# Gated delta rule on one core: places of six small steps and of a recurrence's factors

## The chip, the core and the metric

One NeuronCore of a Trainium2 chip runs the whole program, all in fp32. The metric is the time of one execution on the device in microseconds; three executions of the kernel before were timed. TensorE (PE), VectorE (DVE), ScalarE (ACT), GpSimd (POOL) and SyncE each have a queue of their own and meet only through semaphores.

## What is computed

The reference is a chain of four residual blocks: a gated delta-rule attention, a mixture of experts, a banded attention, and a two-layer local attention. Only the first is touched. Its core, for 4 sequences of 1024 tokens, 16 heads, and 64 keys by 64 values:

```
def step(S, inp):
    qt, kt, vt, at, bt = inp
    err = jnp.einsum('bhij,bhj->bhi', S, kt) - vt
    S = at[..., None] * S - bt[..., None, None] * (err[..., None] * kt[:, :, None, :])
    o = jnp.einsum('bhij,bhj->bhi', S, qt)
    return (S, o)
...
mu = o.mean(-1, keepdims=True)
var = ((o - mu) ** 2).mean(-1, keepdims=True)
o = (o - mu) / jnp.sqrt(var + EPS) * ln_w + ln_b
g = jax.nn.sigmoid(x @ Wg.T).reshape(Bb, Tt, H, DV)
o = (o * g).reshape(Bb, Tt, H * DV)
return o @ Wo.T
```

## The kernel before

`DeltaRule` cuts the 1024 tokens into 32 segments (`SEG` = 32), each into two chunks (`CK` = 16 steps), each chunk into halves (`HC` = 8). A chunk g = 2s + ch of segment s goes like this:

- TensorE projects, makes the products of keys and queries among themselves (Gram), and what the past gives: `pe_past_state` (from the state) and `pe_past_chunk` (L691, from the chunk before). VectorE turns the result into `P2` (L1292), multiplies its first four columns (`HAND` = 4) by the heads' factors `dk` (L1297, L1363 for the second half) and takes them from the values (L1302; the second half adds, L1366).
- VectorE then does the steps t = 1 to 15: a product of the history `H` with a Gram row in PSUM (L1327), a decay (L1331, with the gates' copy `abank` in PSUM) and a sum (L1333). For t from 4 to 7 the decay is GpSimd's (`pool_history`).
- Between the halves stands `dve_cross`: VectorE turns the history (L1348), TensorE multiplies it (`pe_cross`, L709), and VectorE turns the product (L1361). While TensorE works, VectorE does other things: the mean or the deviation of the segment before (L1271), the gates' turn `dve_gates` (L1247, first chunk) or the Gram's turn (L1263, second chunk), and the output's turn (L1281).
- `dve_state` ends the chunk: it turns the history (L1389), which releases L691 for the next chunk, and makes the last output (L1391 to L1398).
- The state sum `dve_add` (L1375, two instructions) stands in the first chunk at step t = 4, the reciprocal (L1276) in the second chunk at t = 11.

Each engine's queue is an order written out by hand (`tensor`, `scalar`, `gpsimd`, `vector`). TensorE's projections share two PSUM banks as a ring: `take` waits until what is two places ahead in the ring has been evacuated. The mean and the deviation use bank 4. The time rows (`pe_time_rows`, L604, two halves) stand at the head of a segment, ahead of the gate's projections; ScalarE evacuates them at L871. GpSimd makes `dk` in `pool_prepare` (L1063, L1065), behind four state decays (L1012) and much else; ScalarE copies Gram rows (`act_gram_bank`, L891, L892) and gates (`act_gate_rows`, L880) to PSUM banks 2 and 3 when the last product of a chunk (L1391) has been made.

## Time and profile before

| | |
|---|---|
| median of three timed executions | 3798.79 us (3794.1 to 3808.33) |
| the profiled execution | 3802.33 us, of which 3800.5 us from its first to its last instruction |
| mean granted TensorE clock | 0.926 |
| PE busy | 3221.9 us (85%) |
| DVE busy | 2951.2 us (78%) |
| ACT busy | 1981.8 us (52%) |
| POOL busy | 2230.6 us (59%) |

The delta rule's recurrence fills the first 2260 us; the other blocks follow. Busy time counts instructions on an engine, not its waits. In a row of the trace, the number in square brackets is the idle time of the engine just before the instruction, and what ended it. A clock of 1.00 is 2.4 GHz and 0.50 is 1.2 GHz; a value between is a mean over a stretch.

### The profile page before, as it was taken

How to read it: one execution, taken by the hardware profiler on the slowest of the kernel's cores; microseconds unless marked ns; L12 is line 12 of the kernel's file. 1: busy time of each engine (PE TensorE's matmuls, PEld its weight loads, DVE VectorE, ACT ScalarE, POOL GpSimd, SP SyncE). 2: the span in 40 equal slices, each digit the busy share in tenths (PEclk: the TensorE clock that was granted, in tenths of full speed). 3: DMA queues.
4: the chain of work that ended last, by engine and by line, in shares of the span. 5: the costliest groups of instructions: out<-in, count | busy, mean ns of one | idle time of the engine just before them, and what ended most of it. 6: DMA issues, size and time to landing. Idle time of an engine off the chain costs nothing. (4 is left out here: it accounts for less than half of the span.)

```text
span 3800.5 us, 141833 instructions
## 1 busy us (share of the span) xinstructions
PE 3221.9 (85%) x61117; PEld 2418.8 (64%) x61117; DVE 2951.2 (78%) x6533; ACT 1981.8 (52%) x4486; POOL 2230.6 (59%) x2825
## 2 busy tenths in 40 slices
PE   3688898888888888889888845689999799889989
PEld 2567676767767676767677644556666477656765
DVE  4488888888888888889888942178888688738884
ACT  2434444444444444444444323258887699629972
POOL 1377778787877777787877744320101388418860
PEclk7889999999999998999999966899999899999999
DMA  2111111111111111111111115100000012101111
GB/s 76 34 43 41 35 52 30 52 34 45 42 45 42 45 41 37 50 30 49 31 40 40 40 31 149 40 1 2 2 2 2 23 35 44 29 20 29 43 32 28
DMA packets 156019, 141.03 MB, mean 37 GB/s; under 512 B 64976, under 2 KB 108236, under 8 KB 155138
## 3 DMA queue, kind: packets, MB, share of 16 engines
q1 hardware_dynamic: 153090, 129.25, 12.5%
q8 instruction: 482, 7.90, 0.9%
...
q14 instruction: 143, 1.17, 0.1%
...
## 5 line engine op out<-in xcount | busy, mean ns | idle before, releaser
L1327 DVE TENSOR_TENSOR a_tmp<-a_h,banks 128x128 f32<-128x128 f32 (+6 forms) x896 | 435.7, 486 | 28.7
L1333 DVE TENSOR_REDUCE a_h<-a_tmp 128x64 f32<-128x128 f32 (+6 forms) x896 | 432.1, 482 | 8.8
L1012 POOL TENSOR_TENSOR a_st<-a_st,a_ab 128x512 f32<-128x512 f32 x252 | 313.6, 1277 | 0.0
L820 ACT ACTIVATE a_kq<-banks 128x512 f32<-128x512 f32 (+2 forms) x160 | 88.3, 552 | 426.6 <-PE banks L556 426.6
L2207 ACT ACTIVATE c_s<-c_s,c_low 128x384 f32<-128x384 f32 (+1 forms) x512 | 266.3, 579 | 19.1 <-DVE c_low L2151 13.6
L1027 POOL TENSOR_TENSOR a_h<-a_h,a_a 128x128 f32<-128x128 f32 (+3 forms) x256 | 141.3, 552 | 228.4 <-DVE a_h L1333 225.6
L2252 POOL TENSOR_TENSOR c_qm<-c_qT,c_heads 128x512 f32<-128x512 f32 x32 | 33.3, 1040 | 396.2 <-PE banks L2076 395.9
L2151 DVE CUSTOM_DVE_ANT_0 c_s<-banks,c_band 128x384 f32<-128x384 f32 (+1 forms) x512 | 245.4, 517 | 23.5 <-PE banks L2076 23.5
L556 PE MATMUL banks<-a_xseg,a_w_q 128*128 128x128 f32 x2048 | 253.4, 278 | 9.0 <-ACT a_kq L820 8.5
L556 PE MATMUL banks<-a_xseg,a_w_k 128*128 128x128 f32 x2048 | 243.0, 276 | 17.1 <-DMA a_xseg<-xn 17.1
L556 PEld LDWEIGHTS banks<-a_xseg,a_w_q 128*128 128x128 f32 x2048 | 235.8, 190 | 21.6 <-ACT a_kq L820 15.4
L556 PEld LDWEIGHTS banks<-a_xseg,a_w_k 128*128 128x128 f32 x2048 | 237.1, 193 | 17.9 <-issue 17.6
L829 ACT ACTIVATE a_va<-banks 128x512 f32<-128x512 f32 x128 | 136.8, 1095 | 208.5 <-PE banks L569 208.0
L569 PE MATMUL banks<-a_w_v,a_xseg 128*32 128x512 f32 x2048 | 242.1, 610 | 0.5 <-issue 0.3
L2090 PE MATMUL banks<-k_ident,c_s 128*128 128x128 f32 x1408 | 216.6, 283 | 28.7 <-ACT c_pt L2214 15.8
L691 PE MATMUL banks<-a_wt,a_gn 32*32 32x64 f32 x8064 | 152.1, 237 | 102.1 <-DVE a_wt L1389 98.9
L709 PE MATMUL banks<-a_wt,a_gx 32*32 32x64 f32 x8192 | 164.3, 244 | 84.9 <-DVE a_wt L1348 72.3
L2090 PEld LDWEIGHTS banks<-k_ident,c_s 128*128 128x128 f32 x1408 | 154.3, 142 | 119.8 <-ACT c_s L2207 113.6
L691 PEld LDWEIGHTS banks<-a_wt,a_gn 32*32 32x32 f32 x8064 | 139.1, 120 | 134.5 <-DVE a_wt L1389 129.7
L709 PEld LDWEIGHTS banks<-a_wt,a_gx 32*32 32x32 f32 x8192 | 151.3, 125 | 93.1 <-issue 89.1
L2588 ACT ACTIVATE d_S<-d_S,d_low 128x128 f32<-128x128 f32 x512 | 199.2, 399 | 19.0 <-DVE d_low L2653 18.7
L2437 PE MATMUL banks<-d_wqkv,d_hT 128*128 128x512 f32 x384 | 199.0, 633 | 11.2 <-DVE d_rot L2635 6.7
...
## 6 DMA issues: line engine op xcount, KB each, us to landing
a_ab<-decays SPq DMA_DIRECT2D x512, 128.0 KB, 3.1
d_Vs<-d_V SPq DMA_DIRECT2D x128, 128.0 KB, 2.4
...
a_xrow<-in_L_attn_x SPq DMA_DIRECT2D x128, 16.0 KB, 1.8
x<-a_xrow SPq DMA_DIRECT2D x128, 16.0 KB, 1.8
...
```

What stands on the lines that cost most here:

```text
L556: t = e.matmul(b[:, m * SW:(m + 1) * SW].rearrange("p (b t) -> p b t", b=NB), self.wT[n][:, j, ct * P:(ct + 1) * P], xs[:, :, off:off + SE ...
L569: t = e.matmul(b[bi * SEG:(bi + 1) * SEG, :], xs[:, bi, off:off + SEG], self.wT[n][:, j, part], start=(j == 0), stop=(j == taps - 1))
L691: t = e.matmul(pb[rows, at:at + DK], self.Gn[1 - ch][rows, 8 * par + ct, :], self.Wt[rows, x:x + 2, :].rearrange("p h i -> p (h i)"), star ...
L709: t = e.matmul(xb[rows, at:at + DK], self.Gx[rows, 8 * par + ct].rearrange("p t z -> p (t z)"), self.Wt[rows, x:x + 2, :].rearrange("p h i ...
L1012: e.tensor_tensor(sv, sv, self.ab[:, 8 * n:8 * n + 8, :], ALU.mult).then_inc(*self.s_decay.at((g, n)))
L1327: e.tensor_tensor(prod, both, gram, ALU.mult).then_inc(*step.at((g, t, "product")))
L1333: e.tensor_reduce(self.results(ch, t), prod, AX.X, ALU.add).then_inc(*step.at((g, t, "w")))
L2090: t = e.transpose(b[:, j * P:(j + 1) * P], self.S[u % self.NS][:, j * P:(j + 1) * P], self.c.ident[:])
L2151: e.tensor_tensor_reduce(out=self.S[u % self.NS][:, 0:w], in0=self.c.bank(r)[:, 0:w], in1=self.W.band[:, m0:m0 + w], scale=-HD ** -0.5, sc ...
L2207: e.activation(s[:, 0:w], s[:, 0:w], ACT.Exp, scale=-1.0, bias=self.low[u % self.NS][:, 0:1]).then_inc(*self.s_exp.at(u))
L2437: e.matmul(b, self.hT[:, g * P:(g + 1) * P], self.W.wqkv[:, z * INNER:(z + 1) * INNER], start=True, stop=True).then_inc(*self.s_proj.at((g ...
L2588: t = e.activation(s, s, ACT.Exp, scale=-1.0, bias=self.low[g % 2][:, par, r:r + 1], accum_out=self.rows[g % 2][:, par, r:r + 1])
```

## The change

What it does, in the order of the diff:

- `H` has its parts in another order, and the results of a step are written output first. Gram rows lie in bank 2 in the order that goes with it, and only the half of each row that is read is copied.
- The factors for the first four columns of each half go to PSUM: ScalarE copies them from `dk` to the free halves of bank 2 (`act_factors`, two instructions for each chunk, ahead of the Gram rows). VectorE's four small instructions each take one operand from PSUM, and the two multiplications also write to PSUM (`scaled`, a free part of bank 3), so that VectorE waits for the gates' copy already there. GpSimd's `pool_prepare` waits for the factors' copy in place of VectorE's multiplications.
- The time rows stand in two places of the second chunk: half 0 behind the next segment's Gram product and ahead of `pe_cross`, half 1 between the past state and the second half of the value projection; the last segment has none.
- The mean's product takes a place in the bank ring and no longer waits for the state sum.
- On VectorE, the state sum stands behind the first chunk's L1348, the gates' turn at the end of the first chunk's `dve_state`, and the reciprocal behind the Gram's turn in the second chunk's `dve_cross`.

```
@@ -474,8 +474,8 @@
...
             self.H = sb("h", [P, 32, 2 * SEG + 2 * CK])
-            self.W = [self.H[:, :, ch * SEG:(ch + 1) * SEG] for ch in range(NCK)]
-            self.Wx, self.O = self.H[:, :, 2 * SEG:2 * SEG + CK], self.H[:, :, 2 * SEG + CK:]
+            self.O, self.Wx = self.H[:, :, 0:CK], self.H[:, :, CK + 2 * SEG:]
+            self.W = [self.H[:, :, CK + ch * SEG:CK + (ch + 1) * SEG] for ch in range(NCK)]
             self.ab = sb("ab", [P, R, DK])
@@ -501,6 +501,7 @@
...
+        self.s_factor = sig("factor")
         self.s_p2, self.s_prep, self.s_step, self.s_wt, self.s_st, self.s_o = (
@@ -511,12 +512,17 @@
...
-        self.gbank = c.bank(2).rearrange("p (t z j) -> p t z j", z=2, j=CK)
+        self.gbank = c.bank(2).rearrange("p (r j) -> p r j", j=CK)
+        self.factor = [self.gbank[:, 2 * HC * h:2 * HC * (h + 1), HC - HC * h:CK - HC * h].rearrange("p r (i t) -> p r i t", t=HAND)
+                       for h in range(2)]
+        self.scaled = c.bank(3)[:, HAND * 32:2 * HAND * 32].rearrange("p (r i t) -> p r i t", i=2, t=HAND)
         self.abank = c.bank(3).rearrange("p (t i) -> p t i", i=32)
...
-        return ch * (SEG + CK) if t <= HAND or t >= HC or (t - HAND) % 2 == 0 else 2 * SEG
+        return CK + (ch * (SEG + CK) if t <= HAND or t >= HC or (t - HAND) % 2 == 0 else 2 * SEG)
@@ -525,8 +531,8 @@
...
-        w, o = self.first_column(ch, t + 1) + t, 2 * SEG + CK + t - 1
-        return self.H[:, :, w:o + 1:o - w].rearrange("p i z -> p z i")
+        w, o = self.first_column(ch, t + 1) + t, t - 1
+        return self.H[:, :, o:w + 1:w - o].rearrange("p i y -> p y i")
@@ -538,7 +544,7 @@
...
         if n >= 2:
-            q.wait_ge(self.s_evac, self.ring[n - 2])
+            q.wait_ge(self.s_moment if self.ring[n - 2][0] == "mean" else self.s_evac, self.ring[n - 2])
         return self.c.bank(n % 2)
@@ -616,16 +622,13 @@
...
-        b = self.c.bank(4)
-        if s + 1 < self.nseg:
-            if which == "mean":
-                q.wait_ge(self.s_st, (s, 3))
-            else:
-                q.wait_ge(self.s_p2, 2 * s + 3)
         if which == "mean":
+            b = self.take(q, ("mean", s))
             q.wait_ge(self.s_o, 2 * s + 1)
         else:
-            q.wait_ge(self.s_moment, ("mean", s))
+            b = self.c.bank(4)
+            if s + 1 < self.nseg:
+                q.wait_ge(self.s_p2, 2 * s + 3)
             q.wait_ge(self.s_squared, s)
@@ -656,7 +659,6 @@
...
             q.wait_ge(self.s_st, (s - 1, 3))
-            q.wait_ge(self.s_moment, ("mean", s - 1))
         if ch == 0 and s >= 2:
@@ -758,8 +760,6 @@
...
                 self.pe_project_rows(e, q, "a", nxt, 1)
-            for n in range(2):
-                self.pe_time_rows(e, q, s, n)
             if older >= 0:
@@ -792,10 +792,12 @@
...
                     self.pe_next_gram(e, q, s, n)
+                self.pe_time_rows(e, q, s, 0)
             self.pe_cross(e, q, s, 1)
...
                 self.pe_past_state(e, q, g + 2)
+                self.pe_time_rows(e, q, s, 1)
                 self.pe_project_rows(e, q, "v", nxt, 1)
@@ -884,12 +886,24 @@
...
         s, ch = divmod(g, 2)
-        js = slice(ch * CK, (ch + 1) * CK)
+        c0, rows = ch * CK, self.g2[:].rearrange("p t z j -> p (t z) j")
         q.wait_ge(self.s_bg, (s, ch))
...
             q.wait_ge(self.s_step, (g - 1, "last", "q"))
-        e.activation(self.gbank[:, 0:CK - 1, 0, :], self.g2[:, 1:CK, 0, js], ACT.Copy)
-        e.activation(self.gbank[:, :, 1, :], self.g2[:, :, 1, js], ACT.Copy).then_inc(*self.s_gbank.at(g))
+        e.activation(self.gbank[:, 0:2 * HC - 2, 0:HC], rows[:, 1:2 * HC - 1, c0:c0 + HC], ACT.Copy)
+        e.activation(self.gbank[:, 2 * HC:2 * CK - 1, HC:], rows[:, 2 * HC + 1:, c0 + HC:c0 + CK], ACT.Copy).then_inc(*self.s_gbank.at(g))
+    def by_pairs(self, x):
+        return x.rearrange("p (r i) t -> p r i t", i=2)
+    def act_factors(self, e, q, g):
+        q.wait_ge(self.s_dk, (g, 1))
+        if g:
+            q.wait_ge(self.s_step, (g - 1, "last", "q"))
+        for h in range(2):
+            t = e.activation(self.factor[h], self.by_pairs(self.dk[:, :, h * HC:h * HC + HAND]), ACT.Copy)
+        t.then_inc(*self.s_factor.at(g))
@@ -944,6 +958,7 @@
...
         self.act_cross_gram(e, q, 0)
+        self.act_factors(e, q, 0)
         self.act_gram_bank(e, q, 0)
@@ -954,8 +969,6 @@
...
                     self.act_project_rows(e, q, "a", nxt, half)
-            for n in range(2):
-                self.act_time_rows(e, q, s, n)
             if older >= 0:
@@ -967,6 +980,7 @@
...
                     self.act_project(e, q, "q", nxt, part)
+            self.act_factors(e, q, g + 1)
             self.act_gram_bank(e, q, g + 1)
@@ -981,13 +995,15 @@
...
                     self.act_next_gram(e, q, s, n)
+                self.act_time_rows(e, q, s, 0)
             if old >= 0:
...
                 self.act_cross_gram(e, q, nxt)
-                for half in range(2):
-                    self.act_project_rows(e, q, "v", nxt, half)
-            if more:
+                self.act_project_rows(e, q, "v", nxt, 0)
+                self.act_time_rows(e, q, s, 1)
+                self.act_project_rows(e, q, "v", nxt, 1)
+                self.act_factors(e, q, g + 2)
                 self.act_gram_bank(e, q, g + 2)
@@ -1035,7 +1051,7 @@
...
     def past_part(self):
-        return self.H[:, :, SEG:SEG + CK]
+        return self.H[:, :, CK + SEG:CK + SEG + CK]
@@ -1044,7 +1060,7 @@
...
         q.wait_ge(self.s_wm, 2 * s + 1)
-        e.tensor_tensor(self.past_part(), self.H[:, :, 0:CK], by, ALU.mult).then_inc(*self.s_past.at(s))
+        e.tensor_tensor(self.past_part(), self.W[0][:, :, 0:CK], by, ALU.mult).then_inc(*self.s_past.at(s))
@@ -1057,9 +1073,8 @@
...
         if g:
-            q.wait_ge(self.s_prep, (g - 1, "mul"))
+            q.wait_ge(self.s_factor, g - 1)
             q.wait_ge(self.s_rest, (g - 1, "late"))
-            q.wait_ge(self.s_mid, (g - 1, "mul"))
         e.tensor_tensor(halves(self.dk[:])[:, :, :, 1:], halves(self.dc[s % 2][:, :, ch * CK:(ch + 1) * CK])[:, :, :, 0:HC - 1],
@@ -1268,7 +1283,8 @@
...
             q.wait_ge(self.s_root, s - 1)
-        e.tensor_reduce((self.mom if which == "mean" else self.var)[:], self.c.bank(4)[:, 0:P].rearrange("p (i t) -> p t i", t=SEG),
+        b = self.held(("mean", s)) if which == "mean" else self.c.bank(4)
+        e.tensor_reduce((self.mom if which == "mean" else self.var)[:], b[:, 0:P].rearrange("p (i t) -> p t i", t=SEG),
                         AX.X, ALU.add).then_inc(*self.s_moment.at((which, s)))
@@ -1292,18 +1308,18 @@
...
         q.wait_ge(self.s_p2, g)
-        q.wait_ge(self.s_dk, (g, 1))
-        first = P2[:, :, 0:HAND, 0]
-        e.tensor_tensor(first, first, self.dk[:, :, 0:HAND], ALU.mult).then_inc(*self.s_prep.at((g, "mul")))
+        q.wait_ge(self.s_factor, g)
+        q.wait_ge(self.s_abank, g)
+        pairs = self.by_pairs
+        e.tensor_tensor(self.scaled, pairs(P2[:, :, 0:HAND, 0]), self.factor[0], ALU.mult).then_inc(*self.s_prep.at((g, "mul")))
         q.wait_ge(self.s_prep, (g, "mul"))
...
             q.wait_ge(step, (g - 2, "last", "o"))
-        e.tensor_tensor(Wc[:, :, c0:c0 + HAND], self.bv[:, :, c0:c0 + HAND], first,
+        e.tensor_tensor(pairs(Wc[:, :, c0:c0 + HAND]), pairs(self.bv[:, :, c0:c0 + HAND]), self.scaled,
                         ALU.subtract).then_inc(*self.s_prep.at((g, "sub")))
...
         q.wait_ge(self.s_gbank, g)
-        q.wait_ge(self.s_abank, g)
         for t in range(1, CK):
@@ -1311,14 +1327,12 @@
...
             both = hist[:, :, lo:t + 1].rearrange("p (o i) j -> p o i j", o=1).broadcast_to([P, 2, 32, t + 1 - lo])
-            gram = self.gbank[:, t - 1, :, lo:t + 1].rearrange("p z (o j) -> p z o j", o=1).broadcast_to([P, 2, 32, t + 1 - lo])
+            gram = self.gbank[:, 2 * t - 2:2 * t, lo:t + 1].rearrange("p y (o j) -> p y o j", o=1).broadcast_to([P, 2, 32, t + 1 - lo])
             if t == lo + 1 and lo:
...
             if t == HAND:
-                if ch == 0 and s:
-                    self.dve_add(e, q, s - 1)
                 q.wait_ge(self.s_rest, (g, "sub", 1))
@@ -1331,13 +1345,11 @@
...
             e.tensor_reduce(self.results(ch, t), prod, AX.X, ALU.add).then_inc(*step.at((g, t, "w")))
-            if ch == 1 and t == 11 and s:
-                self.dve_reciprocal(e, q, s - 1)
...
-        g, x = 2 * s + ch, self.X[:, :, HC:HC + HAND, 0]
+        g, pairs = 2 * s + ch, self.by_pairs
         q.wait_ge(self.s_step, (g, HC - 1, "w"))
@@ -1346,13 +1358,14 @@
...
         e.transpose(self.Wt[:].rearrange("p x i -> p i x"), self.W[ch]).then_inc(*self.s_wm.at(g))
+        if ch == 0 and s:
+            self.dve_add(e, q, s - 1)
         if s:
             self.dve_moment(e, q, s - 1, "dev" if ch else "mean")
-        if s + 1 < self.nseg:
-            if ch:
-                self.dve_gram_rows(e, q, s + 1)
-            else:
-                self.dve_gates(e, q, s + 1)
+        if ch and s + 1 < self.nseg:
+            self.dve_gram_rows(e, q, s + 1)
+        if ch and s:
+            self.dve_reciprocal(e, q, s - 1)
         if ch == 0 and s >= 2:
@@ -1360,10 +1373,10 @@
...
         q.wait_ge(self.s_xt, g)
-        e.tensor_tensor(x, x, self.dk[:, :, HC:HC + HAND], ALU.mult).then_inc(*self.s_mid.at((g, "mul")))
+        e.tensor_tensor(self.scaled, pairs(self.X[:, :, HC:HC + HAND, 0]), self.factor[1], ALU.mult).then_inc(*self.s_mid.at((g, "mul")))
         q.wait_ge(self.s_mid, (g, "mul"))
         q.wait_ge(self.s_rest, (g, "less"))
-        e.tensor_tensor(self.history(ch, HC)[:, :, HC:HC + HAND], self.P2[:, :, HC:HC + HAND, 0], x, ALU.add).then_inc(
+        e.tensor_tensor(pairs(self.history(ch, HC)[:, :, HC:HC + HAND]), pairs(self.P2[:, :, HC:HC + HAND, 0]), self.scaled, ALU.add).then_inc(
             *self.s_mid.at((g, "add")))
@@ -1387,7 +1400,7 @@
...
             e.transpose(self.Wt[:].rearrange("p x i -> p i x"), Wc).then_inc(*self.s_wt.at(g))
-        gq = self.gbank[:, CK - 1, 1, HC:].rearrange("p (o j) -> p o j", o=1).broadcast_to([P, 32, HC])
+        gq = self.gbank[:, 2 * CK - 2, HC:].rearrange("p (o j) -> p o j", o=1).broadcast_to([P, 32, HC])
         e.tensor_tensor(self.tmp[:, 1, :, 0:HC], Wc[:, :, c0 + HC:row], gq, ALU.mult).then_inc(*self.s_step.at((g, "last", "q")))
@@ -1396,8 +1409,8 @@
...
         e.tensor_tensor(o2[:, :, c0:row], self.P2[:, :, :, 1], self.O, ALU.subtract).then_inc(*self.s_o.at(g))
-        if ch and more:
-            self.dve_values(e, q, s + 1)
+        if more:
+            (self.dve_values if ch else self.dve_gates)(e, q, s + 1)
```

## Rows read from the trace of the kernel before

**Rows 1.** Recurrence: length, busy PE, PEld, DVE, ACT, POOL, clock, DMA share, GB/s.
```profile
138.70:2260.00 2121.30, 1821.12 (x47378) 1460.49 (x47367) 1835.58 (x3421) 908.01 (x1673) 1614.13 (x2199) 0.93 0.14 41
```

**Rows 2.** VectorE by line, recurrence: busy us, mean ns | idle before us.
```profile
L1361 DVE STREAM_TRANSPOSE a_cross<-banks 128x1024 f32<-128x1024 f32 x64 | 79.9, 1249 | 127.7 <-PE banks L709 127.7
L1292 DVE STREAM_TRANSPOSE a_p<-banks 128x1024 f32<-128x1024 f32 x64 | 79.3, 1240 | 43.1 <-PE banks L691 43.1
L1302 DVE TENSOR_TENSOR a_h<-a_bv,a_p 128x128 f32<-128x128 f32 x64 | 58.0, 907 | 2.2
...
L1297 DVE TENSOR_TENSOR a_p<-a_p,a_dk 128x128 f32<-128x128 f32 x64 | 39.4, 616 | 2.2
...
L1366 DVE TENSOR_TENSOR a_h<-a_p,a_cross 128x128 f32<-128x128 f32 x64 | 30.9, 483 | 2.2
L1363 DVE TENSOR_TENSOR a_cross<-a_cross,a_dk 128x128 f32<-128x128 f32 x64 | 27.2, 426 | 2.2
...
L1276 DVE RECIPROCAL a_mom<-a_mom 128x32 f32<-128x32 f32 x32 | 11.0, 343 | 0.4 <-ACT a_mom L904 0.4
```

**Rows 3.** VectorE in order of time, one segment: start us, us, [idle before].
```profile
1005.91 1.24 DVE L1247 STREAM_TRANSPOSE a_a<-a_va 128x1024 f32<-128x1024 f32 x1
...
1008.79 1.25 DVE L1361 STREAM_TRANSPOSE a_cross<-banks 128x1024 f32<-128x1024 f32 x1 [0.52 <-PE banks L709]
...
1014.14 0.29 DVE L1331 TENSOR_TENSOR a_h<-a_h,banks 128x128 f32<-128x128 f32 x1
...
1024.38 1.25 DVE L1292 STREAM_TRANSPOSE a_p<-banks 128x1024 f32<-128x1024 f32 x1 [1.39 <-PE banks L691]
...
1032.92 0.62 DVE L1333 TENSOR_REDUCE a_h<-a_tmp 128x64 f32<-128x448 f32 x1
...
1035.02 1.94 DVE L1348 STREAM_TRANSPOSE a_wt<-a_h 128x1024 f32<-128x1024 f32 x1
...
1040.43 1.25 DVE L1361 STREAM_TRANSPOSE a_cross<-banks 128x1024 f32<-128x1024 f32 x1 [2.24 <-PE banks L709]
1041.72 0.90 DVE L1363 TENSOR_TENSOR a_cross<-a_cross,a_dk 128x128 f32<-128x128 f32 x1
...
1056.99 1.25 DVE L1292 STREAM_TRANSPOSE a_p<-banks 128x1024 f32<-128x1024 f32 x1 [0.54 <-PE banks L691]
1058.27 0.91 DVE L1297 TENSOR_TENSOR a_p<-a_p,a_dk 128x128 f32<-128x128 f32 x1
...
1062.42 1.29 DVE L1375 TENSOR_TENSOR a_st<-a_st,banks 128x512 f32<-128x512 f32 x2
```

**Rows 4.** TensorE in order of time, the same segment.
```profile
1006.74 1.99 PE L709 MATMUL banks<-a_wt,a_gx 32*32 32x64 f32 x128
...
1037.11 3.28 PE L709 MATMUL banks<-a_wt,a_gx 32*32 32x64 f32 x128 [2.30 <-DVE a_wt L1348]
...
1053.90 3.04 PE L691 MATMUL banks<-a_wt,a_gn 32*32 32x64 f32 x128 [2.34 <-DVE a_wt L1389]
...
1062.12 2.02 PE L604 MATMUL banks<-k_ident,a_kq 128*32 128x128 f32 x64 [0.50 <-ACT a_va L829]
```

**Rows 5.** Window sums of the two L709 stretches; the clock stands third from the end.
```profile
1006.70:1008.80 2.10, 2.10 (x130) 1.97 (x130) 1.58 (x3) 0.65 (x1) 1.83 (x3) 1.00 0.04 8
1037.10:1040.40 3.30, 3.29 (x132) 3.13 (x136) 1.09 (x1) 0.30 (x1) 3.30 (x4) 0.57 0.02 5
```

**Rows 6.** GpSimd in order of time, second half of the same segment.
```profile
1037.51 4.96 POOL L1012 TENSOR_TENSOR a_st<-a_st,a_ab 128x512 f32<-128x512 f32 x4
...
1054.23 0.31 POOL L1065 COPY a_dk<-a_beta 128x64 f32<-128x64 f32 x1
1056.52 2.51 POOL L1166 TENSOR_TENSOR a_bv<-a_bv,a_beta 128x512 f32<-128x512 f32 x2 [1.99 <-DVE a_bv L1255]
```

**Rows 7.** ScalarE in order of time, the same segment.
```profile
1033.60 0.28 ACT L899 ACTIVATE a_orow<-banks 128x128 f32<-128x128 f32 x1
...
1054.81 0.79 ACT L880 ACTIVATE banks<-a_a 128x96 f32<-128x96 f32 x2
```

More of the change, by code:

```diff
@@ L540, in take @@
         if n >= 2:
-            q.wait_ge(self.s_evac, self.ring[n - 2])
+            q.wait_ge(self.s_moment if self.ring[n - 2][0] == "mean" else self.s_evac, self.ring[n - 2])
         return self.c.bank(n % 2)
@@ L760, in tensor @@
                 self.pe_project_rows(e, q, "a", nxt, 1)
-            for n in range(2):
-                self.pe_time_rows(e, q, s, n)
             if older >= 0:
@@ L886, in act_gram_bank @@
         s, ch = divmod(g, 2)
-        js = slice(ch * CK, (ch + 1) * CK)
+        c0, rows = ch * CK, self.g2[:].rearrange("p t z j -> p (t z) j")
         q.wait_ge(self.s_bg, (s, ch))
@@ L956, in scalar @@
                     self.act_project_rows(e, q, "a", nxt, half)
-            for n in range(2):
-                self.act_time_rows(e, q, s, n)
             if older >= 0:
@@ L987, in scalar @@
                 self.act_cross_gram(e, q, nxt)
-                for half in range(2):
-                    self.act_project_rows(e, q, "v", nxt, half)
-            if more:
+                self.act_project_rows(e, q, "v", nxt, 0)
+                self.act_time_rows(e, q, s, 1)
+                self.act_project_rows(e, q, "v", nxt, 1)
+                self.act_factors(e, q, g + 2)
                 self.act_gram_bank(e, q, g + 2)
@@ L1270, in dve_moment @@
             q.wait_ge(self.s_root, s - 1)
-        e.tensor_reduce((self.mom if which == "mean" else self.var)[:], self.c.bank(4)[:, 0:P].rearrange("p (i t) -> p t i", t=SEG),
+        b = self.held(("mean", s)) if which == "mean" else self.c.bank(4)
+        e.tensor_reduce((self.mom if which == "mean" else self.var)[:], b[:, 0:P].rearrange("p (i t) -> p t i", t=SEG),
                         AX.X, ALU.add).then_inc(*self.s_moment.at((which, s)))
```

92 lines of the change are left out of this document (51 added, 41 removed).

## The prediction

> **What bounds the kernel now.** I read the page's busy shares first, then the recurrence alone. It runs from 138.7 to 2260 us, 2121 us for 32 segments, 66.3 us each, and VectorE is busy 1835.6 us of it, TensorE 1821.1 us and GpSimd 1614.1 us [rows 1]. Next I read VectorE's groups by line, for the idle time ahead of them and for the mean of each. Nearly all of the idle time stands at two lines: 127.7 us ahead of L1361 (turn of the cross product, called X here) and 43.1 us ahead of L1292 (turn of the past product, called P), both released by TensorE. Beside that, four small instructions have means that don't fit their size: L1297, L1302, L1363 and L1366 all handle 128x128, and take 616, 907, 426 and 483 ns [rows 2].
>
> Then one segment in VectorE's order of time, from some 1004 to 1068 us. It has four waits: X in the first chunk 0.52 us, P in the second 1.39, X in the second 2.24, P of the next first chunk 0.54 [rows 3]. TensorE's part of the same stretch shows why the two late ones last: it waits 2.30 us for the turned history and then needs 3.28 us for the 128 small matmuls of L709, which took 1.99 us where no wait stood before them; L691 takes 3.04 us behind a wait of 2.34 [rows 4]. The granted clock was 0.57 in the slow stretch and 1.00 in the quick one, that is, mostly the 1.2 GHz level against the 2.4 GHz level [rows 5]. And the four odd instructions follow GpSimd: L1297 ends at 1059.18, 0.15 us after GpSimd's L1166 pair (1056.52 + 2.51); L1363 ends at 1042.62, 0.15 us after GpSimd's four decays (1037.51 + 4.96) [rows 3, 6]. L1331 on the same 128x128, with one operand in PSUM, took 0.29 us at 1014.14, an ordinary time for it [rows 3]. So the bound is VectorE's own chain, lengthened by TensorE's answers and by GpSimd's hold on it.
>
> **The four small instructions.** All become: one operand in SBUF, one in PSUM (two of them write PSUM too). Nearest row: L1331 at 0.29. The four groups sum to 39.4 + 58.0 + 27.2 + 30.9 = 155.5 us [rows 2]; 256 x 0.29 = 74.2; to gain at most 81.3 us. No arithmetic of the trace writes PSUM from VectorE. Bounds: 0.29 each, or 0.43 each (the next step that these lines show, as in L1366's 483 mean), which would cost 36 us more; I take 0.29, since L1331 has the same size and a PSUM operand.
>
> The Trainium skill speaks against this: "VectorE: DVE Perf Modes", section on the TRN2 errata, gives a PSUM source 120 fixed cycles against 58 for SBUF, an estimate of 0.065 us more for each, 17 us in all. The trace doesn't agree: 0.29 for L1331.
>
> **The waits.** In the first chunk, behind L1348, the state sum (L1375, a pair in 1.29 us) takes the place of the gates' turn (L1247, 1.24 us) [rows 3]. VectorE's cover ahead of X stays 2.75 us; the wait goes because L709 starts on time. Before, the projections ahead of it ran past L1348; the two L604 groups now taken out of this stretch were 2.02 us and 0.50 of waiting for ScalarE [rows 4]. With 0.15 + 1.99 us the product is there before the cover ends. Mean in the bank ring only takes the wait for the state sum off TensorE, which would otherwise stand in front of the mean; its price is that the turn two slots later waits for VectorE's L1271, about 1.5 us behind L1348, while TensorE is still at L709: nothing. Turn 0 does wait about 0.6 us for L1281, which stands behind the state sum; TensorE has about that much to spare before L691.
>
> The gates' turn goes to the end of the first chunk's state step, in the wait of 1.39 us before P: 0.15 left [rows 3]. L691's product is usually there in 2.1 us, in this segment in 2.8, and the cover is now 2.8. Who is behind it: GpSimd's cumulation (first used 7 us later) and the "v" projections' evacuation.
>
> In the second chunk, the reciprocal (L1276, 0.34 us [rows 2]) moves ahead of X, and L604's first half (1.0 us) fills TensorE's wait of 2.30 before L709, the second half part of the 2.34 before L691 [rows 4]. What is left of each is about what TensorE had at other places without the clock falling, so I take 1.99 us for both products. X then comes 2.1 us behind L1348 instead of 3.4. A new wait appears: the evacuation of the time rows now stands on ScalarE ahead of the table load and the square root, so the reciprocal waits about 0.5 us; X starts 1.17 us earlier instead of 1.6.
>
> **What is late next.** From the end of step 6 of the second chunk (1032.92 + 0.62 = 1033.54) to L1297 of the next chunk (1058.27) VectorE now takes 24.73 us [rows 3]. Without 1.17 at X, 0.54 at P and 0.75 at L1363 and L1366 it would take 22.3. But GpSimd runs without a break from the same point to the end of L1065 (1054.54), 21.0 us [rows 6]. In the change ScalarE starts its factor copies only then, two at 0.28 (L899, 128x128), the two halved Gram copies at 0.28, and the gate rows at 0.79 [rows 7]: 1.9 us. VectorE waits for all of them ahead of its first multiplication, since `scaled` lies in the gate rows' bank. 21.0 + 1.9 = 22.9. L1398 still has two operands in SBUF and now falls among GpSimd's instructions; bounds 0 and 0.69, I add 0.4: 23.3. So this stretch goes from 24.73 to 23.3 and not to 21.2, the sum of all its idle and held time: 2.1 us for each segment aren't given back.
>
> On L1398 the Trainium skill, "SBUF — State Buffer", section on the two separate sides, says that whichever of the two engines comes first holds the shared port for its whole instruction. By that rule the 0.4 would be 0.69, 9 us more in all. No row shows L1398 beside GpSimd.
>
> In the first chunk's stretch L1065 is 2 us earlier than needed and ScalarE's chain fits.
>
> **The sum.** Idle 127.7 + 43.1 and held 81.3 make 252 us. Off: 31 x 2.1 = 65 for GpSimd's chain; 9 for the first and last segment, whose waits have no neighbour's work to fill them (an estimate, two segments of 4.7); 4 for what passes the gates' cover; 7 for a lower clock at the first chunk's L709 in a third of the segments (0.15 + 3.28 - 2.75 = 0.7 each, and TensorE now waits ahead of it). 252 - 65 - 9 - 4 - 7 = 167. The profiled execution took 3802.3 us (span 3800.5), 3.5 above the median of 3798.8, so 3802.3 - 167 = **3635 us**. Nothing behind 2260 us is touched.
>
> **Rivals.**
> A. An instruction with one SBUF operand still waits for GpSimd, so the factors in PSUM do nothing. For: GpSimd's decays ran through every chunk and VectorE's transposes of SBUF can't be told from free ones. Against: L1331 at 0.29 amid the decays. The 81 us stay, of which 0.75 a segment (23) lay under GpSimd's chain anyway: 109 us of gain, 3693.
> B. The low clock stays or moves to the first chunk's products. For: TensorE still waits a microsecond at each place. Then the second chunk's stretch takes 24.73 - 0.34 - 0.75 = 23.6 against 23.3, and X and P of the two other places cost 0.7 + 0.35: 1.35 x 31 less the 7 counted, 35 us less: 3670.
> C. GpSimd's chain isn't the limit, because it too is freed of the held instructions and ScalarE needs less: the stretch takes 22.3, 31 us more gain: 3604.
> D. **Slower**: ScalarE's chain behind L1065. Every microsecond that the factor copies take above 0.56 counts in the second chunk's stretch, and in the first chunk's behind a slack of 1.8. With c us more it costs c + c - 1.8, and eats the 5.4 us of gain per segment from c = 3.6, that is, 2.1 us a copy. At c = 4.0 it is 6.2 against 5.4: 25 us slower, 3827. Against: no ScalarE copy of this size takes over 0.28 [rows 7].
>
> **Chances.** Forecast 0.56, A 0.14, B 0.13, C 0.12, D 0.05. The range takes in A, B and C with the ends of the unknown costs: 3598 to 3698. A measurement here can tell about 0.5% (19 us) from no change; faster by more 0.94, within 0.02, slower by more 0.04.
>
> **What would show it.** Right: the means of the four small groups at 290 ns; idle ahead of P near nothing in the second chunk; idle ahead of X under 40 us in all; L709 and L691 at 2 us with clock 1.00; VectorE waiting about 1 us, for ScalarE's gate rows (L880's successor), ahead of the first multiplication of each first chunk. Wrong: means of 400 to 900 (A), X of the second chunk still 2 us late (B), no wait at the first multiplication (C), factor copies over 1 us (D).

## The result

The changed kernel takes 3685.96 us (3683.97 to 3692.4) against 3798.9 us (3794.1 to 3808.33) for the kernel before, a ratio of 0.9699 with a 95% interval of 0.9679 to 0.972: 113 us faster. Its profiled execution spans 3682.8 us, at a mean granted clock of 0.946 where it was 0.926. The forecast was 3635 us, a gain of 164 us against the median, in a range of 3598 to 3698. So the direction and the range held, and 51 us of the gain didn't come.

The recurrence shrank from 2121.3 to 2003.3 us. Window sums of the kernel after over that stretch (length; busy PE, PEld, DVE, ACT, POOL with instruction counts; clock; DMA share; GB/s), which answer [rows 1]:

```profile
138.70:2142.00 2003.30, 1769.59 (x47296) 1411.82 (x47288) 1767.87 (x3421) 919.45 (x1798) 1611.52 (x2199) 0.97 0.15 43
```

VectorE's groups by line in the kernel after, recurrence (busy us, mean ns | idle us before them and what ended it), which answer [rows 2]. L1374 is X, L1308 is P; L1314, L1319, L1376 and L1379 are the four small instructions (L1297, L1302, L1363, L1366 before); L1292 is the reciprocal:

```profile
L1374 DVE STREAM_TRANSPOSE a_cross<-banks 128x1024 f32<-128x1024 f32 x64 | 79.9, 1248 | 62.7 <-PE banks L711 62.3
L1308 DVE STREAM_TRANSPOSE a_p<-banks 128x1024 f32<-128x1024 f32 x64 | 77.6, 1213 | 3.6 <-PE banks L693 3.4
L1411 DVE TENSOR_TENSOR a_o<-a_p,a_h 128x512 f32<-128x512 f32 x64 | 51.5, 804 | 2.2
...
L1314 DVE TENSOR_TENSOR banks<-a_p,banks 128x128 f32<-128x128 f32 x64 | 18.9, 296 | 4.0 <-ACT banks L882 1.9
L1376 DVE TENSOR_TENSOR banks<-a_cross,banks 128x128 f32<-128x128 f32 x64 | 18.9, 296 | 2.2
L1379 DVE TENSOR_TENSOR a_h<-a_p,banks 128x128 f32<-128x128 f32 x64 | 18.4, 287 | 2.2
L1319 DVE TENSOR_TENSOR a_h<-a_bv,banks 128x128 f32<-128x128 f32 x64 | 18.3, 287 | 2.2
L1292 DVE RECIPROCAL a_mom<-a_mom 128x32 f32<-128x32 f32 x32 | 11.3, 353 | 57.1 <-ACT a_mom L918 57.1
```

The four small groups fell from 155.5 to 74.5 us (-81.0), the idle time ahead of P from 43.1 to 3.6 (-39.5), that ahead of X from 127.7 to 62.7 (-65.0). Against them stands a new wait: 57.1 us ahead of the reciprocal, for ScalarE's square root, where it was 0.4. L1411, with both operands in SBUF still, grew by 7.2 us from this row of the kernel before:

```profile
L1398 DVE TENSOR_TENSOR a_o<-a_p,a_h 128x512 f32<-128x512 f32 x64 | 44.3, 692 | 2.2
```

-81.0 - 39.5 - 65.0 + 56.7 + 7.2 = -121.6; the recurrence is 118.0 us shorter. In this sum 56.7 is the rise of the reciprocal's wait (57.1 less 0.4).

One segment of the kernel after in VectorE's order of time (start us, us, [idle before and what ended it]), which answers [rows 3]:

```profile
985.51 2.00 DVE L1360 STREAM_TRANSPOSE a_wt<-a_h 128x1024 f32<-128x1024 f32 x1
...
990.22 0.35 DVE L1292 RECIPROCAL a_mom<-a_mom 128x32 f32<-128x32 f32 x1 [1.49 <-ACT a_mom L918]
...
991.28 1.25 DVE L1374 STREAM_TRANSPOSE a_cross<-banks 128x1024 f32<-128x1024 f32 x1 [0.72 <-PE banks L711]
...
1007.71 0.30 DVE L1314 TENSOR_TENSOR banks<-a_p,banks 128x128 f32<-128x128 f32 x1
...
1021.26 1.25 DVE L1374 STREAM_TRANSPOSE a_cross<-banks 128x1024 f32<-128x1024 f32 x1 [0.71 <-PE banks L711]
...
1036.41 1.21 DVE L1308 STREAM_TRANSPOSE a_p<-banks 128x1024 f32<-128x1024 f32 x1
```

Both P come without a wait. But X of the second chunk starts 3.77 us behind the end of L1360 (987.51 to 991.28), where it was 3.47 (1036.96 to 1040.43 [rows 3]) and should have become 2.3, that is 3.47 less the 1.17 of the prediction. TensorE in the same segment shows why:

```profile
986.80 1.08 PE L610 MATMUL banks<-k_ident,a_kq 128*32 128x128 f32 x32
987.82 1.42 PE L711 MATMUL banks<-a_wt,a_gx 32*32 32x64 f32 x87
990.45 0.77 PE L711 MATMUL banks<-a_wt,a_gx 32*32 32x64 f32 x41 [1.21 <-issue]
...
1003.94 1.99 PE L693 MATMUL banks<-a_wt,a_gn 32*32 32x64 f32 x128 [0.92 <-DVE a_wt L1402]
...
1010.00 0.57 PE L737 MATMUL banks<-a_wt,a_kt 32*64 32x64 f32 x22 [1.14 <-issue]
...
1019.20 1.99 PE L711 MATMUL banks<-a_wt,a_gx 32*32 32x64 f32 x128
```

The matmuls of L711 run at full clock now, 87 in 1.42 us and 41 in 0.77, but 1.21 us lie between them in which TensorE waits for nothing that the profile shows ("issue"). The totals of that kind in the recurrence, by the line in front of which they stand, first of before, then of after (us, times, longest):

```profile
PE banks L735 <- issue: 16.7, 14, 2.1
PE banks L709 <- issue: 12.5, 10, 2.0
```

```profile
PE banks L711 <- issue: 29.9, 30, 2.2
PE banks L737 <- issue: 26.4, 28, 1.9
```

L711 is L709 before, L737 is L735. The clock's loss was traded for a gap of this kind: all 30 gaps at L711 stand in the second chunk's product, one in each of 30 segments out of 32, where it was 9 before. On the mean of all segments this product takes 3.24 us from its first to its last matmul (3.45 before), and it starts 0.90 us behind the end of VectorE's turn (0.41 before). So it arrives no earlier. By chunk the idle time ahead of X is 34.4 us in the first (40.6 before) and 28.3 us in the second (87.2 before), and in the second the reciprocal's 57.1 us come on top: 85.4 us in place of 87.2 + 0.4.

ScalarE ahead of the reciprocal, the same segment:

```profile
987.95 0.60 ACT L873 ACTIVATE a_kt<-banks 128x512 f32<-128x512 f32 x1 [0.63 <-PE banks L610]
988.57 1.28 ACT L918 ACT_TABLE_LOAD   x1
989.86 0.32 ACT L918 ACTIVATE a_mom<-a_variance,k_eps 128x32 f32<-128x32 f32 x1
```

The time rows' evacuation comes 0.4 us behind the end of L1360, and the table load and the square root follow it.

### The profile page after: what moved, and what is told of

Same layout as the page of the kernel before. It is cut to its first block and busy times, and to the rows that moved or that the text cites. A ratio compares the mean times of both kernels' runs of the same rounds, so it can differ in the third digit from the quotient of the medians.

```text
span 3682.8 us, 141831 instructions
## 1 busy us (share of the span) xinstructions
PE 3171.1 (86%) x61053; PEld 2370.2 (64%) x61053; DVE 2884.4 (78%) x6533; ACT 1993.4 (54%) x4612; POOL 2227.9 (60%) x2825
## 5 line engine op out<-in xcount | busy, mean ns | idle before, releaser
L1347 DVE TENSOR_REDUCE a_h<-a_tmp 128x64 f32<-128x128 f32 (+6 forms) x896 | 431.8, 482 | 8.8
L831 ACT ACTIVATE a_va<-banks 128x512 f32<-128x512 f32 x128 | 138.4, 1099 | 163.1 <-PE banks L575 162.6
L1345 DVE TENSOR_TENSOR a_h<-a_h,banks 128x32 f32<-128x32 f32 (+6 forms) x640 | 175.0, 273 | 21.9
L711 PE MATMUL banks<-a_wt,a_gx 32*32 32x64 f32 x8192 | 140.5, 220 | 52.1 <-issue 29.9
L2741 POOL TENSOR_TENSOR d_sw<-d_raw,d_tab 128x256 f32<-128x256 f32 x256 | 178.3, 729 | 0.0
L693 PE MATMUL banks<-a_wt,a_gn 32*32 32x64 f32 x8064 | 130.3, 217 | 46.4 <-DVE a_wt L1402 43.2
```

The costliest lines, as they stand in the source:

```text
L1345: e.tensor_tensor(hist[:, :, lo:t], hist[:, :, lo:t], at, ALU.mult).then_inc(*step.at((g, t, "decay")))
L1347: e.tensor_reduce(self.results(ch, t), prod, AX.X, ALU.add).then_inc(*step.at((g, t, "w")))
L2741: e.tensor_tensor(self.heads(sw[:, z, :])[:, :, a * hf:(a + 1) * hf], self.heads(raw[:, z, :])[:, :, (1 - a) * hf:(2 - a) * hf], sn, ALU.m ...
```

## The experiments

All ratios are to the kernel before, on the same chip. Two theories were tested: that the terms of the sum are what they were said to be, and **theory T/S**, that TensorE follows VectorE so closely that a filled wait is given back at the next product (T), the more so as it runs out of instructions in its dense stretches (S). "First" and "second chunk" behind an idle time mean that part of it, added up from the rows of the trace.

**1. The factors alone.** The kernel before, with only the order of `H` and of the Gram rows, `act_factors`, `factor` and `scaled` of the diff.

> The kernel before with only the factors in PSUM (and the order of H and of the Gram rows that goes with it); state sum, gates' turn, reciprocal, mean and time rows as before. In the changed kernel the four small groups fell from 155.5 to 74.5 us. Theory T, TensorE follows VectorE so closely that a shorter VectorE only makes it wait longer for TensorE: a gain of 40 to 65 us, with the four groups at 75 us and the idle time ahead of the two turned products 15 to 40 us above 171. Rival, held time comes back in full: a gain of 75 to 85 us and idle time unchanged. Rival, GpSimd's chain is the limit: a wait for ScalarE ahead of the first multiplication of 0.5 us or more a segment.

Ratio 0.9767 (0.9723 to 0.981), 3731.62 against 3808.61 us. The idle time ahead of X and P, of this kernel:

```profile
L1380 DVE STREAM_TRANSPOSE a_cross<-banks 128x1024 f32<-128x1024 f32 x64 | 80.0, 1250 | 133.1 <-PE banks L715 133.1
L1311 DVE STREAM_TRANSPOSE a_p<-banks 128x1024 f32<-128x1024 f32 x64 | 78.6, 1229 | 32.2 <-PE banks L697 32.2
```

165.3 us of idle time where it was 170.8, and 0.0233 x 3808.61 = 89 us of gain (72 to 105 by the interval). The four executions of this kernel lie 31 us apart, though: by the medians the gain is 77 us, and the profiled one, the slowest, is 61 us shorter than that of the kernel before. In it the state sum waits 14.5 us (4.5 before) and the first multiplication 6.4 (2.2 before). So most of the held time came back, and whether all of it did isn't settled. The 15 to 40 us more of idle time ahead of the two turned products that theory T foresaw aren't there.

**2. The same instructions in SBUF.** The changed kernel, with

```
+            self.fs, self.ss = sb("fs", [P, 2, 32, HAND]), sb("ss", [P, HAND * 32])
...
-        self.factor = [self.gbank[:, 2 * HC * h:2 * HC * (h + 1), HC - HC * h:CK - HC * h].rearrange("p r (i t) -> p r i t", t=HAND)
-                       for h in range(2)]
-        self.scaled = c.bank(3)[:, HAND * 32:2 * HAND * 32].rearrange("p (r i t) -> p r i t", i=2, t=HAND)
+        self.factor = [self.fs[:, h].rearrange("p (r i) t -> p r i t", i=2) for h in range(2)]
+        self.scaled = self.ss[:].rearrange("p (r i t) -> p r i t", i=2, t=HAND)
```

> The changed kernel with its factors and the scaled product in SBUF tiles in place of PSUM: the same instructions in the same order, only their memory differs. Theory P, an instruction with both operands in SBUF is held until GpSimd's running instruction ends: the four small groups go back from 74.5 to over 130 us, and the time up by 40 us or more. Rival, it is the new order, the pairs' layout or the copy into a tile of its own that made them quick: the groups stay under 85 us and the time within 10 us of the changed kernel.

Ratio 0.9839 (0.9824 to 0.9854), 3744.41 against 3804.79 us. Its four small groups:

```profile
L1319 DVE TENSOR_TENSOR a_h<-a_bv,a_ss 128x128 f32<-128x128 f32 x64 | 70.3, 1099 | 2.2
...
L1379 DVE TENSOR_TENSOR a_h<-a_p,a_ss 128x128 f32<-128x128 f32 x64 | 38.4, 600 | 2.2
...
L1314 DVE TENSOR_TENSOR a_ss<-a_p,a_fs 128x128 f32<-128x128 f32 x64 | 28.7, 448 | 2.2
...
L1376 DVE TENSOR_TENSOR a_ss<-a_cross,a_fs 128x128 f32<-128x128 f32 x64 | 26.4, 412 | 2.2
```

163.8 us against 74.5, with nothing changed but the memory. It is the second operand in SBUF that holds them. The time is 1.4% above that of the changed kernel (0.9839 against 0.9699), some 53 us, less than the 89 us of the groups: the wait for the square root is 24 us shorter here (33.1 us) and L1411 6.2 us (45.3), while the idle time ahead of X is 7.8 us longer (70.5).

**3. VectorE's moves alone.** The kernel before, with the state sum, the gates' turn and the reciprocal in their new places and the mean in the ring.

> The kernel before with only VectorE's three moves and the mean in the bank ring. From the rows of before: the second chunk's waits ahead of L1292 (28.8 us in all) are filled by the gates' turn, and the reciprocal's 11 us go into the wait ahead of L1361. Theory T: 30 to 40 us of gain. Rival, TensorE answers to whatever VectorE does first, so a filled wait comes back at the next product: under 20 us.

Ratio 1.0001 (0.9983 to 1.0018), 3807.82 against 3808.61 us: nothing. Its X and P:

```profile
L1356 DVE STREAM_TRANSPOSE a_cross<-banks 128x1024 f32<-128x1024 f32 x64 | 80.0, 1249 | 131.0 <-PE banks L705 131.0
L1289 DVE STREAM_TRANSPOSE a_p<-banks 128x1024 f32<-128x1024 f32 x64 | 78.6, 1228 | 22.2 <-PE banks L687 22.1
```

```profile
L1273 DVE RECIPROCAL a_mom<-a_mom 128x32 f32<-128x32 f32 x32 | 10.5, 328 | 10.7 <-ACT a_mom L900 10.7
```

P fell by 21 us, and X rose by 3. By chunk, X rose from 40.6 to 68.1 us in the first and fell from 87.2 to 62.8 in the second, where the reciprocal now stands and itself waits 10.7 us for the square root (0.4 before). The profiled execution was the quickest of ten, and its gain (11.7 us of span) isn't in the timed runs. The first chunk's L705 starts 2.44 us behind the end of VectorE's turn, where L709 before started 1.39 behind it: TensorE is late there, and VectorE only came sooner. So a filled wait was given back at the next product. That is theory T as it stands above; the recorded expectation has the names the other way round and calls it the rival.

**4. The time rows alone.** The kernel before, with the time rows in their two places on TensorE and ScalarE.

> The kernel before with only the time rows in their two new places. The step of the prediction: both of the second chunk's products run at full clock and TensorE is on time for the first chunk's, 60 to 80 us of gain. Theory T, now that the changed kernel's trace shows TensorE idle for 'issue' 91 us where it was 51: the denser stretches ahead of the two products run out of instructions, and the gain is 25 to 50 us, with 15 to 40 us more idle for issue than before.

Ratio 0.9877 (0.985 to 0.9904), 3768.14 against 3808.61 us, 47 us.

```profile
L1361 DVE STREAM_TRANSPOSE a_cross<-banks 128x1024 f32<-128x1024 f32 x64 | 79.3, 1238 | 96.7 <-PE banks L709 96.7
L1292 DVE STREAM_TRANSPOSE a_p<-banks 128x1024 f32<-128x1024 f32 x64 | 78.6, 1229 | 31.2 <-PE banks L691 31.2
```

X gave 31 us, 21 of them in the first chunk (40.6 to 19.4) and only 10 in the second (87.2 to 77.3), where all of the loss to the clock should have gone. TensorE's gaps for issue rose to 80 us in all from 51, at L735 to 27.0 from 16.7, as theory T expected. Against the gain stands more held time: the four small groups, still in SBUF, take 172.1 us here, 16.6 more than before. The three parts give 89 + 0 + 47 = 136 us by the ratios; together they gave 113. By the medians the parts give 77 + 1 + 40 = 118, so that the parts don't add up isn't shown.

**5. The reciprocal back.** The changed kernel, with

```
+            if ch == 1 and t == 11 and s:
+                self.dve_reciprocal(e, q, s - 1)
...
-        if ch and s:
-            self.dve_reciprocal(e, q, s - 1)
```

> The changed kernel with the reciprocal back at step 11 of the second chunk. In the changed kernel it waits 57.1 us for ScalarE's square root, and the turned product stands behind it. Theory W, that wait costs only what it reaches past the product's arrival, which is late as well: with the reciprocal back, 11 us are added to the chain and some 57 us of wait show as idle ahead of the turned product instead; the time is within 10 us of the changed kernel. Rival, the wait is on the path: 35 to 50 us faster than the changed kernel.

Ratio 0.9653 (0.9618 to 0.9689), 3675.7 against 3808.61 us. By the ratios it is 0.5% better than the changed kernel, some 17 us, though the intervals just overlap. In the second chunk the idle time ahead of X is 96.5 us, which is what idle time, wait and reciprocal were together in the changed kernel (28.3 + 57.1 + 11.3 = 96.7): all of it lay in front of a product that was late in any case. So the wait itself cost nothing there, and the move gained nothing. At step 11 the reciprocal takes its 11 us again, and the idle time ahead of X fell by as much in the first chunk, from 34.4 to 22.8 us: VectorE comes later there, to a product that is late.

**6. Fewer instructions ahead of L711.** As 5, and in `pe_next_gram`, for the second half:

```
-        for ct in range(NCT):
+        for n in range(6 * par):
+            t = e.matmul(b[:, 0:P], self.c.ident[:], self.c.ident[:], start=True, stop=True)
+        for ct in range(0 if par else NCT):
```

This kernel leaves out half of the next segment's Gram product, so it serves only to measure.

> The changed kernel with the reciprocal back at step 11, and the second of the next segment's two Gram products (L600, 64 matmuls of 32 columns, 0.66 us) replaced by 6 products of 128 columns with about the same time on TensorE; so half of that product is left out. Theory S, the gap of 0.97 us inside L711 is TensorE running out of instructions behind three groups of many small ones: with 116 instructions fewer ahead of it the gap falls under 0.5 us on average and the second chunk's idle time ahead of the turned product from 96 us to under 82. Rival L, it is just late and slow whatever stands before it: the gap stays at 0.8 to 1.1 us.

TensorE's gaps in front of that product, first of 5, then of this kernel (L713 is L711 there):

```profile
PE banks L711 <- issue: 30.2, 30, 2.1
```

```profile
PE banks L713 <- issue: 1.6, 3, 1.1
```

```profile
L1376 DVE STREAM_TRANSPOSE a_cross<-banks 128x1024 f32<-128x1024 f32 x64 | 79.6, 1244 | 94.6 <-PE banks L713 94.5
```

The gaps are gone. In the trace 64 matmuls of 0.7 us in all, each with its weight load, have become 12 with theirs, 104 instructions fewer and not 116; and the 12 take 1.60 us, so TensorE has 0.9 us more to do there and not the same. L713 starts later for it, 1.27 us behind VectorE's turn on the mean where L711 in kernel 5 starts 0.86 behind, and yet is done sooner, since it takes 2.14 us in place of 3.28. In the second chunk the idle time ahead of X fell from 96.5 to 72.9 us. This is what theory S foresaw; that it is instructions that TensorE lacks is shown in the last section. Fewer instructions and more time for each were changed together here. The ratio was 0.9595 (0.9566 to 0.9625), two executions, 3661.75 against 3813.63 us, 0.6% below kernel 5, with intervals that just overlap.

**7. and 8. The first half of the time rows behind the last q projection.**

```
                 self.pe_project(e, q, "q", nxt, 2)
+                self.pe_time_rows(e, q, s, 0)
...
-                self.pe_time_rows(e, q, s, 0)
             self.pe_cross(e, q, s, 1)
```

and ScalarE's evacuation likewise, ahead of the square. Kernel 7 has the reciprocal back at step 11, kernel 8 has it in the changed kernel's place.

> The changed kernel with the reciprocal back at step 11, and the first half of the time rows behind the last q projection, where TensorE waits 0.7 us for ScalarE in any case (22 us in all), instead of directly ahead of L711. Theory S and that free place together: L711 starts 0.5 to 0.7 us earlier and 64 matmuls fewer stand in the dense stretch: 15 to 30 us faster than the kernel with the reciprocal back (ratio 0.957 to 0.961). Rival L: the wait for ScalarE only moves and L711 ends as late as before, within 8 us.

> The changed kernel with nothing else than the first half of the time rows behind the last q projection; the reciprocal stays ahead of the turned product. The square root no longer waits behind the time rows' evacuation. Theory W, the reciprocal's wait of 57.1 us came from that place: it falls under 20 us, and the kernel is 0 to 11 us faster than the same with the reciprocal at step 11 (0.9599), so 0.957 to 0.960. Rival: the square root is late for another reason, the wait stays over 35 us and the ratio over 0.962.

Kernel 7: 0.9599 (0.9571 to 0.9626), 3657.69 against 3813.63 us. Kernel 8: 0.9613 (0.9591 to 0.9635), 3655.96 against 3804.79 us. Its reciprocal:

```profile
L1292 DVE RECIPROCAL a_mom<-a_mom 128x32 f32<-128x32 f32 x32 | 11.6, 363 | 3.4 <-ACT a_mom L918 3.3
```

The wait fell from 57.1 to 3.4 us. So it came from the evacuation in front of the table load, as foreseen, and the reciprocal's place makes no difference that can be told. Kernel 8's ratio is a little above the 0.957 to 0.960 that were expected. Against 5, kernel 7 is 0.5% faster, with intervals that just overlap; in its second chunk the idle time ahead of X fell from 96.5 to 61.8 us, since L711 starts 0.15 us behind VectorE's turn in place of 0.86 and takes 2.92 us in place of 3.28. Within it gaps of 15 us in all remain.

**9. TensorE's work spread otherwise.** As 5, with one half of the a projection behind `pe_carry`, and

```
-PARTS = {"k": ((0, 4), (4, 8)), "q": ((0, 2), (2, 5), (5, 8)), "g": ((0, 4), (4, 8))}
+PARTS = {"k": ((0, 4), (4, 8)), "q": ((0, 3), (3, 6), (6, 8)), "g": ((0, 4), (4, 8))}
```

> The changed kernel with the reciprocal back, and TensorE's work spread otherwise: the first half of the a projection (1.06 us) from the stretch ahead of the first chunk's L711 to the one ahead of L693, and one of eight q tiles (1.0 us) from the second chunk's stretch to the first's. Both stretches that lose work end late by 0.8 and 0.7 us, both that gain it have 0.5 to 0.8 us idle. Theory B, TensorE's lateness is what is left of the waits: 30 to 45 us faster than with the reciprocal back (ratio 0.953 to 0.957). Rival G, GpSimd's chain of 21.7 us and ScalarE's 1.6 us then set the second chunk's stretch: under 15 us, and a wait for ScalarE's gate rows ahead of the first multiplication.

Ratio 0.9706 (0.9685 to 0.9726), 3701.51 against 3813.63 us: 20 us slower than 5, and both theories missed. In the second chunk, which lost a q tile, the idle time ahead of X fell from 96.5 to 82.1 us. But it rose from 22.8 to 45.9 us in the first chunk, and ahead of P from 2.6 to 15.2. TensorE in this kernel waits 34.0 us for issue at L737, 27.9 us for ScalarE's a rows ahead of the g projection and 10.1 us for P ahead of L737. The two edits weren't tried apart, so which of them did it stays open.

**10. The state sum back at step 4.** As 5.

> The changed kernel with the reciprocal back, and the state sum (1.29 us) back at step 4 of the first chunk. Theory T, ahead of the first chunk's L711 TensorE is late by 0.84 us, so there the state sum costs only what reaches past that: the idle time ahead of the first chunk's turned product stays within 15 us of 23 and the time goes up by 0 to 15 us. The prediction's step: the sum is on the path at step 4 and hidden behind L1348: 30 to 39 us slower.

Ratio 0.9715 (0.9695 to 0.9735), 3705.4 against 3813.63 us: 24 us slower than 5, between the two expectations. The idle time ahead of the first chunk's X is 45.9 us where it was 22.8, and theory T had it within 15 us of 23. Once the time rows are out of the way, 24 of the state sum's 39 us are on the path.

**11. The Gram product split.** As 8, with the output's 16 large matmuls between the two halves of `pe_next_gram`.

> As the kernel with the time rows behind the q projection, and the output's 16 large matmuls between the two halves of the next segment's Gram product, so that 64 small matmuls fewer stand directly ahead of L711. Theory S, instruction supply: the gap inside L711 falls from 0.48 us to under 0.25 and the time by 3 to 10 us against its neighbour in this call. Rival: with a wait of 1.3 us ahead of L711 the supply has recovered anyway, and the clock falls instead; within 3 us.

Ratio **0.9569** (0.9556 to 0.9582), 3641.41 against 3804.79 us, the best of all, 0.4% below kernel 8 (on the same chip) and 1.3% below the changed kernel by the ratios. TensorE's gaps at L711 and VectorE's first multiplication in this kernel:

```profile
PE banks L711 <- issue: 9.1, 9, 1.6
```

```profile
L1316 DVE TENSOR_TENSOR banks<-a_p,banks 128x128 f32<-128x128 f32 x64 | 18.9, 296 | 15.3 <-ACT banks L883 13.8
```

The 0.4% are 17 us, more than the 3 to 10 that theory S foresaw. The idle time ahead of X is 53.2 us (90.3 in kernel 8), and now VectorE waits 13.8 us for ScalarE's gate rows behind GpSimd's chain, the bound that the prediction named.

**12. The gates' turn back, in 11.**

> The kernel with the split Gram product (0.9569), with the gates' turn (1.24 us) back behind the first chunk's L1348, where the state sum now stands as well. The prediction's step: the turn fills the wait ahead of the second chunk's L1308, which comes back at 25 to 30 us in all, and in its old place it delays the first chunk's turned product by what reaches past that product's arrival, 1.1 us less the 0.7 us of idle time that it finds there: 20 to 30 us slower. Theory T, TensorE follows and is late for both: what the turn costs at one place it gives back at the other, 0 to 10 us slower.

Ratio 0.9607 (0.9591 to 0.9624), 3659.42 against 3807.2 us: 0.4% slower than 11 by the ratios, 14 us, between the two expectations. Its P, X and reciprocal:

```profile
L1310 DVE STREAM_TRANSPOSE a_p<-banks 128x1024 f32<-128x1024 f32 x64 | 78.6, 1228 | 32.2 <-PE banks L693 32.2
L1379 DVE STREAM_TRANSPOSE a_cross<-banks 128x1024 f32<-128x1024 f32 x64 | 79.0, 1234 | 44.9 <-PE banks L711 44.6
L1294 DVE RECIPROCAL a_mom<-a_mom 128x32 f32<-128x32 f32 x32 | 11.3, 353 | 14.2 <-ACT a_mom L919 14.2
```

The wait ahead of P is 32.2 us against 4.4 in kernel 11. At X 8.3 us came back (44.9 against 53.2), and the reciprocal waits 7.3 us longer (14.2 against 6.9). The profiled executions are 26.6 us apart, the timed ones 14: these rows don't show where the difference between the two went.

## Why the prediction was right, and where it was short

- **The four small instructions.** Right, to 0.3 us: 81.3 forecast, 81.0 measured; alone 89 us of time by the ratio (72 to 105), 77 by the medians. L1331 at 0.29 us was the proper neighbour, also for the two that write PSUM (296 ns; the two that write SBUF take 287). The extra of 0.065 us each, an estimate from the Trainium skill, "VectorE: DVE Perf Modes", section on the TRN2 errata, didn't show. Rival A is out by these means and by experiment 2.
- **P.** Right: 43.1 to 3.6 us. That it was worth as much in time wasn't: alone the moves gave nothing (3), in the best kernel the gates' turn gave 14 us (12). The step left out that VectorE only comes sooner to the next product, for which TensorE was late (by chunk, in 3).
- **X, the step that failed.** The sum left some 45 us of wait ahead of X and the reciprocal (about 1.1 us in each second chunk for the product and the square root, 7 us at the first chunk's, and the outer segments); the trace has 119.8, of which 85.4 in the second chunk and 34.4 in the first. Two terms were mis-sized.
  "I take 1.99 us for both products", and both start on time: right for L693, and the clock did stay up, but L711 in the segment above stretched to 3.4 us by a gap of 1.21 (987.82 to 991.22). Over all segments it takes 3.24 us, of which 0.93 are such gaps, and it starts 0.90 us late where 0.15 was taken. Gaps of this kind stood in the trace of before 10 times at L709 and I passed over them. I had put L610 in the one place where it lengthens a run of small matmuls, and took the wait that it filled for idle time; it was also time in which TensorE's next instructions could arrive (6, and the last section).
  The second term is the 7 us for a lower clock at the first chunk's L711: it was 34.4 us and had another reason. TensorE isn't on time there; it comes 1.1 us late (1018.09 to 1019.20) at full clock, 1.24 us on the mean of all segments. The gap at L737 stands in that stretch; how much of the lateness is due to it wasn't tried.
- **The reciprocal's wait.** Foreseen at 0.5 us a segment, measured 57.1 us, 1.8 a segment. All of it lay in front of the late product (5). Its cause is as given (8).
- **GpSimd's chain.** The length of the chain was right: the end of step 6 (L1347) stands at 984.03, that of L1080 at 1005.55, that of ScalarE's gate rows at 1007.20, which makes 23.2 us against 23.3 forecast:

```profile
1004.78 0.77 POOL L1080 COPY a_dk<-a_beta 128x64 f32<-128x64 f32 x1
```

```profile
1006.38 0.82 ACT L882 ACTIVATE banks<-a_a 128x96 f32<-128x96 f32 x2
```

In the changed kernel VectorE came later still (1007.71), so the chain set the end in few segments (4.0 us of wait at L1314); in kernel 11, where X is quicker, it does in more of them (15.3 us). The segment shown is a quick one: it takes 23.68 us to 1007.71, but the mean of 30 segments is 24.40, where it was 24.86 before. This stretch gave 0.46 us a segment and not 1.43. Rival C, that it isn't the limit, holds for the changed kernel, though not with its gain: what came in its place was TensorE.
- **The sum.** 167 us forecast, 118 in the profiled executions, 113 in the timed ones. X and the reciprocal cost 75 us more than was left for them, and the wait at the first multiplication, for which about 31 us were left, was 4.0. That makes 48 us, nearly all of the difference. So a part of the 65 us that were taken off for GpSimd's chain paid for TensorE's lateness: that the time lies within the range owes something to luck. It lies nearer to the times of rivals A (3693) and B (3670) than to the forecast. Of the five signs named for "right" two came true, the means of the small groups and the wait ahead of P. X under 40 us and a wait of about 1 us for ScalarE's gate rows didn't, and the products at 2 us and full clock came true for L693 alone. Rival B has the right place (X of the second chunk stays late) by a wrong cause. Rival D is out: the factor copies took 0.48 us as a pair.

## What to carry to other kernels

A wait of an engine that issues many small instructions isn't only idle time; its next instructions arrive in it. Look in the waits for "issue" at the lines that follow it before filling it, and fill it with few, large instructions. Where two engines answer each other in turn, a filled wait counts only if the other engine is on time at the next meeting; price a move there and not where the wait stood. A VectorE instruction with two operands in SBUF beside a busy GpSimd could here be held until GpSimd's running instruction had ended (means of 412 to 1099 ns), and with one of them in PSUM it wasn't (287 to 296 ns).

## What the chip showed

- **Hold between VectorE and GpSimd, both ways.** The copy of L1080 took 0.77 us above, where L1065, the same copy, took 0.31 [rows 6]: L1411 with both operands in SBUF ran from 1004.63 to 1005.39. So 0.46 us came onto the chain, where the prediction had added 0.4. The Trainium skill, "SBUF — State Buffer", section on the two separate sides, has it so: whichever of the two engines starts first keeps the shared port for its whole instruction, and the other is blocked. The trace agrees: L1080 starts 0.61 us before the end of L1411 and ends 0.16 us behind it.
- **TensorE's instructions come in packets, and it waits for them.** Another gap of the kernel after stands in L610:

```profile
1046.35 0.86 PE L610 MATMUL banks<-k_ident,a_kq 128*32 128x128 f32 x22
1048.46 0.60 PE L610 MATMUL banks<-k_ident,a_kq 128*32 128x128 f32 x10 [1.26 <-issue]
```

From 1046 to 1048.5 us the DMA engines moved one packet, of the instruction queue, and nothing else:

```profile
q8 instruction: 1, 0.02, 2.3%
```

That packet isn't in the gap. It ran from 1046.08 to 1047.01; TensorE stopped at 1047.2 and went on at 1048.46, 1.45 us behind the packet's end. The whole trace has it so. In the recurrence 77 gaps for issue are longer than 0.5 us, and 76 of them end 1.2 to 1.65 us behind the end of a packet of this queue; of TensorE's 99 other waits of that length, 3 do. Before, it is 34 of 34 gaps, against some 5% of the other waits. The queue moved 371 packets for TensorE's 94,584 matmuls and weight loads, 255 for each packet, and 358 packets in experiment 6, for 91,427, again 255. So these gaps are waits for TensorE's own instructions. How far ahead they are fetched, and what else sets the time of a packet, wasn't tried.
- **A gap can cost twice.** One of 1.95 us inside L587 was followed by a lower granted clock, 0.76 as the mean of the next 7 us, a part at 1.2 GHz and the rest at 2.4 GHz. In them TensorE did its large matmuls: those of L635 took 3.10 us and those of L647 2.58 us, where they took 2.05 and 1.95 at 1041.33 and 1043.21. The gap of 1.21 us inside L711 wasn't followed by a lower clock (1.00 in the 0.8 us behind it). Why the one was and the other wasn't stays open.

```profile
1171.27 0.42 PE L587 MATMUL banks<-a_kq 64*32 64x64 f32 x12 [1.95 <-issue]
```

```profile
1171.00:1178.00 7.00, 6.73 (x156) 6.51 (x158) 5.89 (x8) 2.62 (x8) 6.55 (x9) 0.76 0.01 2
```
